# Second attention of an eight-image hybrid block: the token norm's root folded into the inner norm, values scaled behind their projection, GpSimd's work tied to the low copy

## What is computed

```python
t = _to_tokens(x)
t = t + _L1_attn_ref(_ln_t(t), ...)      # _ln_t: (v - mean) / sqrt(var + 1e-5), over the 128 channels
t = t + _L1_ffn_ref(_ln_t(t), ...)

def _L1_attn_ref(x, w_qkv, w_proj, qn_w, kn_w):
    EPS = 1e-06
    def _rmsnorm(x, w):
        y = xf * jax.lax.rsqrt(jnp.mean(xf * xf, axis=-1, keepdims=True) + EPS)
        return y * w
    qkv = x @ w_qkv.T
    q = _rmsnorm(heads(q), qn_w)          # mean over the two channels of a head
    k = _rmsnorm(heads(k), kn_w)
    att = jnp.einsum('bhtd,bhsd->bhts', q, k) * scale
    att = jnp.where(causal, att, -1e+30); att = jax.nn.softmax(att, axis=-1)
    return (att @ v) @ w_proj.T
```

## Time and profile before

| | us |
|---|---|
| median of 3 runs | 3653.44 (3650.4 to 3662.63) |
| the profiled execution, its own time | 3642.61 |
| its span in the profile | 3640.9 |
| first exponential of stage D starts | 994.8 |
| its last exponential ends | 3217.2 |

### The profile page before, as it was taken

One profiled execution on the slowest core, in us unless ns is written; L12 is line 12 of the kernel. 1 busy time (PEld: TensorE's weight loads), 2 busy tenths in 40 slices (PEclk: granted clock), 3 DMA queues, 4 the chain that ended last, 5 costly groups with the idle time before them and its releaser, 6 DMA issues.

```text
span 3640.9 us, 71108 instructions
## 1 busy us (share of the span) xinstructions
PE 3182.2 (87%) x27941; PEld 1144.4 (31%) x27941; DVE 2109.2 (58%) x3000; ACT 2727.1 (75%) x2577; POOL 296.9 (8%) x228
## 2 busy tenths in 40 slices
PE   5799999999398898898898898898898888979999
PEld 3344444444122222222222222222222222234443
DVE  3688888887347557457547546646646634432222
ACT  4444444444299999899999999899999999934555
POOL 5100000000200000101101101100100100010000
PEclk9899999999699999999999989999999999978999
DMA  5411212110100200210210200200210121000000
GB/s 186 125 44 50 51 45 49 42 42 11 45 16 17 57 25 19 55 25 16 55 26 18 55 25 16 55 25 18 46 34 16 25 48 43 19 11 6 14 12 14
DMA packets 134480, 136.78 MB, mean 38 GB/s; under 512 B 29102, under 2 KB 113164, under 8 KB 134156
## 3 DMA queue, kind: packets, MB, share of 16 engines
q1 hardware_dynamic: 134156, 132.29, 14.3%
HBM read 70.31 MB, written 55.57 MB: 35 GB/s over the span
## 4 chain that ended last, share of the span: by engine, by line
PE 45%; ACT 24%; issue 15%; DVE 11%; SPq 2%; POOL 2%; DMA 1%; DVEq 0%; ACTq 0%; POOLq 0%
ACT arena L896 23%; PE ps L1207 12%; PE ps L1167 5%; PE ps L1283 3%; PE ps L1290 3%; DVE arena L1591 3%; PE ps L1295 3%; PE ps L968 3%; PE ps L1015 3%; PE ps L1042 2%; PE ps L1017 2%; PE ps L1026 2%; PE ps L997 2%; SPq L499 1%; DVE arena L1373 1%
## 5 line engine op out<-in xcount | busy, mean ns | idle before, releaser
L896 ACT ACTIVATE arena<-ps 128x1536 f32<-128x1536 f32 x1536 | 2080.3, 1609 | 165.7 <-PE ps L1167 165.2
L1207 PE MATMUL ps<-arena 128*32 128x512 f32 (+3 forms) x12288 | 1305.4, 521 | 59.4 <-DVE arena L1591 59.4
L1591 DVE TENSOR_TENSOR arena<-arena,causal 128x512 f32<-128x512 f32 x1024 | 714.4, 739 | 368.5 <-ACT arena L896 359.5
L1167 PE MATMUL ps<-arena 15*128 15x512 bf16 (+3 forms) x6144 | 627.0, 340 | 198.3 <-ACT arena L896 152.8
L1167 PEld LDWEIGHTS ps<-arena 15*128 15x128 bf16 x6144 | 166.5, 92 | 1144.8 <-ACT arena L896 948.5
L840 ACT ACTIVATE arena<-ps 128x512 f32<-128x512 f32 x512 | 299.7, 595 | 267.2 <-PE ps L1017 256.8
L1207 PEld LDWEIGHTS ps<-arena 128*32 128x32 f32 x12288 | 289.2, 111 | 471.8 <-issue 349.1
L1373 DVE TENSOR_REDUCE arena<-ps 128x32 bf16<-128x1024 f32 x256 | 311.3, 1216 | 121.0 <-PE ps L997 121.0
L1380 DVE TENSOR_TENSOR arena<-arena,ps 128x512 f32<-128x512 f32 x512 | 329.2, 679 | 26.9 <-PE ps L1026 25.6
L1576 DVE COPY arena<-ps 128x512 f32<-128x512 f32 x256 | 176.5, 689 | 251.9 <-PE ps L1207 250.7
L1015 PE MATMUL ps<-arena 96*128 96x256 bf16 x1024 | 258.5, 277 | 0.3 <-ACT arena L816 0.2
(11 more groups left out here) (201 smaller groups left out, 2070.2 us busy)
## 6 DMA issues: line engine op xcount, KB each, us to landing
arena<-qstack SPq DMA_DIRECT2D x512, 30.0 KB
parts<-arena SPq DMA_DIRECT2D x8, 1536.0 KB, 5.9
arena<-parts SPq DMA_DIRECT2D x48, 256.0 KB, 5.6
arena<-parts SPq DMA_DIRECT2D x96, 128.0 KB, 2.8
arena<-kstack SPq DMA_DIRECT2D x512, 24.0 KB
qstack<-arena SPq DMA_DIRECT2D x48, 192.0 KB, 2.8
attn<-arena SPq DMA_DIRECT2D x512, 12.0 KB
arena<-arena SPq DMA_DIRECT2D x384, 16.0 KB, 1.8
```

The costliest lines, as they stand in the source:

```text
L896: act.activation(PR1[:, at:at + CW], bank(BPC * (f % 2), BPC), ACT.Exp).then_inc(d_exp, 1)
L1167: mm = pe.matmul(bank(at + k)[:, s * P:(s + n) * P], Ks[par][HR * h:HR * h + QROWS, j * P:(j + 1) * P], Qs[par][HR * h:HR * h + QROWS, t * ...
L1207: mm = pe.matmul(o[HR * h:HR * (h + 1), :], V1[n % 2][:, j, v:v + HR], pr[:, h * HALF + s * P:h * HALF + (s + k) * P], start=not opened[hi ...
L1591: dve.tensor_tensor(v, v, m3, ALU.min).then_inc(d_mask, 1)
```

## The change

With v the variance of a token and s the sum of squares of a head's two *unscaled* projections, the normed query is q / sqrt(s/2 + 1e-6 (v + 1e-5)): the outer root cancels and only its variance, times the inner epsilon, is left. So queries and keys are projected from the centred `xc`, and `vb`, the variance spread over a head's rows by two full matmuls, enters the inner root (`nrm[4]`, `eb`). The root of v is still needed for the values, which are projected from `xc` as well and multiplied by it, per token, when they are read out of bank 6: eight instructions of 128 columns per image in place of two copies of 512. turn, w0, w1 and the two multiplications by the widened root are gone for the next image; the projection side keeps its own.

- The tables are now by slot. Next image: m (group 0), q (1), k (2), vb and the first half of the variance by token (3), its second half (4), v (5). z for the image after next: group 6. The finished image: y (8), z (10), m (11), the variance halves in (12, 1) and (13, 0), turn and w0 (14), w1 and lg (15).
- Newton rounds of both token norms are done by GpSimd, four steps a round, 12 in a chain (`pool_root`); those of the inner norm stay on VectorE.
- `low_copied`: GpSimd waits for the low copy of group 1 before it squares `xc`, of 2 and 3 before queries' and keys' squares, of 9 before the products, of 12 before the squares of the finished image.
- Low planes are made by VectorE in group 11. The windows move up by one or two groups; the one of group 9 has the high planes and the first subtractions.
- SyncE stores the planes in group 11 in place of 12, and loads the attended values in group 0 in place of 2; the reciprocal of the divisors moves from group 4 to 2.
- Scratch space is taken from the planes' own words, behind a wait for their last stores.
- The first image's norm is rewritten to the same algebra; z0, z1 and the residual of image 1 are done in it.

```diff
+C_AT = {(0, 0): "m0", (0, 1): "m1", (1, 0): "q0", (1, 1): "q1", (2, 0): "k0", (2, 1): "k1", (3, 0): "vb",
+        (3, 1): "va0", (4, 0): "va1", (5, 0): "v0", (5, 1): "v1"}
+Z_AT = {(6, 0): "z0", (6, 1): "z1"}
+E_AT = {(8, 0): "y0", (8, 1): "y1", (10, 0): "z0", (10, 1): "z1", (11, 0): "m0", (11, 1): "m1", (12, 1): "va0",
+        (13, 0): "va1", (14, 0): "turn", (14, 1): "w0", (15, 0): "w1", (15, 1): "lg"}
...
+def use(g, slot):
+
+    n, gi = g // GPI, g % GPI
+    if (gi, slot) in C_AT and n + 1 < B:
+        return "C", n + 1, C_AT[gi, slot]
+    if (gi, slot) in Z_AT and n + 2 < B:
+        return "Z", n + 2, Z_AT[gi, slot]
+    if (gi, slot) in E_AT and n > 0:
+        return "E", n - 1, E_AT[gi, slot]
+    return None
...
-                if n + 1 < B and gi == 12:
-                    CG.after(sp, n, "lo3")
+                if n + 1 < B and gi == 11:
+                    CD.after(sp, n, "lo3")
                     store_stacks(n + 1)
...
+            def pool_root(steps, n, p, t_sem, first, v, y, t):
+
+                first()
+                for j in (1, 2, 3):
+                    if j > 1:
+                        steps.after(pool, n, f"{p}y{j - 1}")
+                    pool.tensor_tensor(t, y, y, ALU.mult).then_inc(t_sem, 1)
+                    steps.after(pool, n, f"{p}a{j}")
+                    pool.tensor_tensor(t, t, v, ALU.mult).then_inc(t_sem, 1)
+                    steps.after(pool, n, f"{p}b{j}")
+                    pool.tensor_scalar(t, t, -0.5, 1.5, ALU.mult, ALU.add).then_inc(t_sem, 1)
+                    steps.after(pool, n, f"{p}c{j}")
+                    pool.tensor_tensor(y, y, t, ALU.mult).then_inc(t_sem, 1)
...
+            def low_copied(g):
+
+                pool.wait_ge(d_ev, g * 2 + 1)
+
+            def pool_c(n):
+
+                m, g = n - 1, (n - 1) * GPI
+                low_copied(g + 1)
+                for th in range(2):
+                    CD.after(pool, m, f"xc{th}")
+                    pool.tensor_tensor(sq_h[th], xc_h[th], xc_h[th], ALU.mult).then_inc(c_pool, 1)
+                pool.wait_ge(c_stored, n * C_STORES * INC)
+                for j, last in enumerate(("ssq", "ssk")):
+                    low_copied(g + 2 + j)
+                    for k, to in ((2 * j, xn_h[j]), (2 * j + 1, scratch[j])):
+                        CD.after(pool, m, f"r{k}")
+                        pool.tensor_tensor(to, nrm[k], nrm[k], ALU.mult).then_inc(c_pool, 1)
+                    CG.after(pool, m, f"s{2 * j + 1}")
+                    pool.tensor_tensor(xn_h[j], xn_h[j], scratch[j], ALU.add).then_inc(c_pool, 1)
+                pool_root(CG, m, "d", c_pool, lambda: CD.after(pool, m, "dy0"), dv, dev, dtmp)
+                low_copied(g + 9)
+                CD.after(pool, m, "bound")
+                for k, to in enumerate((spare, xn_h[1])):
+                    pool.tensor_tensor(to, nrm[k], nrm[2 + k], ALU.mult).then_inc(c_pool, 1)
+                CG.after(pool, m, "p1")
+                pool.tensor_tensor(spare, spare, xn_h[1], ALU.add).then_inc(c_pool, 1)
+
             def pool_e(n):
+                if n + 1 < B:
+                    low_copied((n + 1) * GPI + 12)
                 for th in range(2):
                     ED.after(pool, n, f"xc{th}")
                     v = num[:, th * HALF:(th + 1) * HALF]
                     pool.tensor_tensor(esq[:, th * HALF:(th + 1) * HALF], v, v, ALU.mult).then_inc(e_pool, 1)
-
...
+                pool_root(EG, n, "e", e_pool, lambda: ED.after(pool, n, "ey0"), ev, edev, etmp)
...
-            def variance(squares, o, t_sem):
-
-                for t in range(NT):
+            def variance(squares, blocks, o, t_sem):
+
+                for t in blocks:
                     mm = pe.matmul(o[:, t:t + 1], squares[:, t * P:(t + 1) * P], mean_w[:, 0:1], start=True, stop=True)
                 mm.then_inc(t_sem, 1)
+
+            def variance_by_head(o, t_sem):
+
+                for th in range(2):
+                    mm = pe.matmul(o[NH1 * th:NH1 * (th + 1), :], mean_w[:, 0:NH1], sq_h[th], start=True, stop=True)
+                mm.then_inc(t_sem, 1)
...
-                    mm = pe.matmul(o[NH1 * th:NH1 * (th + 1), :], wt("qk1")[:, NH1 * k:NH1 * (k + 1)], xn_h[th],
+                    mm = pe.matmul(o[NH1 * th:NH1 * (th + 1), :], wt("qk1")[:, NH1 * k:NH1 * (k + 1)], xc_h[th],
...
+            def pe_c(n, name, o):
+
+                m = n - 1
+                if name in ("m0", "m1"):
+                    th = int(name[1])
+                    ZD.after(pe, m, f"x{th}")
+                    mean_of(n, th, o, c_pe)
+                elif name in ("q0", "q1", "k0", "k1"):
+                    CD.after(pe, m, "xc1")
+                    queries_keys(("q0", "q1", "k0", "k1").index(name), o, c_pe)
+                elif name == "vb":
                     CG.after(pe, m, "sq1")
-                    variance(sq, o, c_pe)
...
-                    values_of(th, o, c_pe)
+                    variance_by_head(o, c_pe)
+                elif name in ("va0", "va1"):
+                    th = int(name[2])
+                    CG.after(pe, m, "sq1")
+                    variance(sq, range(th * NT // 2, (th + 1) * NT // 2), o, c_pe)
                 else:
...
+                    CD.after(pe, m, "xc1")
+                    values_of(int(name[1]), o, c_pe)
...
+                elif name == "vb":
+                    dve.tensor_scalar(nrm[4], o, LN_EPS, RMS_EPS, ALU.add, ALU.mult).then_inc(c_dve, 1)
+                elif name in ("va0", "va1"):
+                    at = int(name[2]) * NT // 2
+                    dve.tensor_scalar(dv[:, at:at + NT // 2], o[:, at:at + NT // 2], LN_EPS, None, ALU.add)\
+                        .then_inc(c_dve, 1)
+                    if at:
+                        root_first(CD, m, "dv1", c_dve, dv, dev)
                 else:
-                    dve.tensor_copy(nrm[C_READ.index(name) - C_READ.index("r0")], o).then_inc(c_dve, 1)
+                    CG.after(dve, m, "dy3")
+                    for t in range(NT // 2):
+                        at = int(name[1]) * NT // 2 + t
+                        ins = dve.tensor_scalar(V1[n % 2][:, at, 0:3 * NH1].rearrange("p (h e) -> p h e", e=3)[:, :, 0:2],
+                                                o[:, t * P:(t + 1) * P].rearrange("p (h d) -> p h d", d=2),
+                                                dev[:, at:at + 1], None, ALU.mult)
+                    ins.then_inc(c_dve, 1)
...
+                    CD.after(dve, m, "eb")
+                    dve.scalar_tensor_tensor(xn_h[j], xn_h[j], 0.5, nrm[4], ALU.mult, ALU.add).then_inc(c_dve, 1)
+                    root_first(CD, m, p + "v", c_dve, xn_h[j], scratch[2 + j])
+                    root_round(CD, m, p, 1, c_dve, xn_h[j], scratch[2 + j], spare)
...
+                if gi == 3:
                     begun(0)
-                elif gi == 6:
+                elif gi == 4:
                     for j in (2, 3):
-                        root_round(CD, m, "q", j, c_dve, sq_h[0], xc_h[0], spare)
-                elif gi == 7:
+                        root_round(CD, m, "q", j, c_dve, xn_h[0], scratch[2], spare)
+                elif gi == 5:
                     normed(0)
                     normed(1)
+                elif gi == 6:
                     begun(1)
+                elif gi == 7:
+                    for j in (2, 3):
+                        root_round(CD, m, "k", j, c_dve, xn_h[1], scratch[3], spare)
                 elif gi == 8:
-                    for j in (2, 3):
-                        root_round(CD, m, "k", j, c_dve, sq_h[1], xc_h[1], spare)
-                elif gi == 9:
...
-                    CG.after(dve, m, "own")
-                    dve.wait_ge(c_stored, n * C_STORES * INC)
+                    dve.scalar_tensor_tensor(xn_h[0], xn_h[1], cv(c_ck + 1), xn_h[0], ALU.mult, ALU.add).then_inc(c_dve, 1)
+                elif gi == 9:
...
+                elif gi == 11:
+                    for k in five:
+                        CD.after(dve, m, f"mid{k}")
+                        r = hi_plane(k)
+                        dve.tensor_tensor(planes[:, r + 2, :], rst[k], planes[:, r + 1, :], ALU.subtract).then_inc(c_dve, 1)
```

360 lines of the change are left out of this document (159 added, 201 removed).

## The result

| | before | changed |
|---|---|---|
| median, us | 3651.92 (3644.97 to 3662.63, 4 runs) | 3535.28 (3533.61 to 3541.48, 4 runs) |
| profiled execution's span | 3640.9 | 3532.1 |
| stage D: first exponential to the end of the last | 2222.5 | 2121.9 |
| behind it | 423.7 | 426.3 |

The forecast of 3516 with its range of 3477 to 3572 and its sign were right; 19 us of the 136 did not come.

What follows compares the result with a forecast made beforehand. ScalarE's exponentials bound the second attention, with 177 us lost to clock falls and GpSimd-VectorE lock-step. Leaving 43 gains 134, plus 3.4 first norm, less 1.2 tail: 136 off the 3653.4 median, given as 3516 us, range 3477 to 3572.

Steps and rivals of the forecast that it cites:

- Parts 3 and 4: GpSimd held until low copies, low planes to VectorE: groups 5, 6, 10 regain 6.2 us, group 12 6.6, collisions cost 1.0.
- part 4: Low planes made by VectorE in group 11 (3.5 us more there); group 12 loses its 6.6 us excess.
- Parts 1 and 2: Next norm's widening goes, ending 5.7 us excess in groups 3 and 4; halved, moved variance costs 1.0, bounds 0 and 4.3.
- Part 7: Second projection half moved ahead, w1 and logits in group 15: costs 2.5 us an image, from 0 to 4.1 plus 2.9.
- Small misses: Allowance for unpriced loss in the stage: 0.5 us for each of images two to seven.
- Part 9: First norm, done once: the first long reciprocal starts earlier, gaining 3.4 us, bounds 0 and 6.
- Part 6: Token norms' Newton rounds on GpSimd, 0.2 us a step: hidden in the stream, 1.2 us lost in the tail.
- Part 5: Values scaled leaving PSUM, eight instructions of 0.17 to 0.35 us: 0.4 more than now per half, hidden in group 5.
- Part 8: SyncE's plane stores one group earlier, attended values loaded in group 0 instead of 2: cost 0.
- The rival of a clock that keeps falling: Clock falls at variance halves, w1 with logits, and after low-copy waits: 13 us lost per image, 3565 us; chance 0.20.
- Collisions: Rival: held GpSimd work delays masks in groups 3, 4 and 9, 4.2 us each, giving 3604 us; chance 0.05.
- the slow chain: Rival: VectorE in group 5 waits for 12 chained GpSimd Newton steps; at 3.2 us each 3675 us; chance 0.02.

Runs made afterwards that it cites:

- e1: Kernel before with only GpSimd's holds to the low copy added, and a finished image's squares put ahead of the planes: 3596.6 us, ratio 0.9829.
- e2: Changed kernel with GpSimd's waits for the low copy taken out: 3577.7 us, ratio 0.9782.
- e6: Changed kernel with the five low planes' differences back on GpSimd, held to the low copy of group 11: 3534.2 us, ratio 0.9672.
- e13: Kernel of e5 with the next image's variance whole in the second slot of group 4, in place of two halves: 3502.2 us, ratio 0.9598.
- e5: Kernel of e4 with three few-column pieces in groups 4, 13 and 15 moved from first to second slot: 3489.7 us, ratio 0.9551.
- e4: Changed kernel with router logits out of the stream, made once in the tail from images summed on GpSimd: 3519.6 us, ratio 0.9624.
- e10: Changed kernel with the router logits' 16 products 128 columns wide instead of 8, using other weights (output differs): 3517.9 us, ratio 0.9632.
- e9: Changed kernel with transposes in group 13's second slot, w0 and w1 in group 14, only router logits in group 15: 3517.0 us, ratio 0.9625.
- e7: Changed kernel with the three Newton rounds of each token norm back on VectorE: 3536.0 us, ratio 0.9689.
- e12: Kernel of e5 with the Newton rounds of the token norms back on VectorE, as in e7: 3504.7 us, ratio 0.9602.
- e3: Changed kernel with the next image's variance whole in group 4's first slot, in place of two halves: 3550.3 us, ratio 0.9689.

## Why the prediction was right, and where it was not

**Parts 3 and 4, the hold: right, with a wrong split.** 6.2 plus 6.6 less 1.0 was the forecast for an image; e1, with no hold on the products and a fall of the clock left in group 12, gives 7.6, and e2 takes 7.1 away. Groups 5 and 6 fell by 3.7, 10 by 1.5, 12 by 6.6, and the 0.5 each set aside for groups 3 and 9 were not needed. But part 4 gave the whole 6.6 of group 12 to the low planes and their move to VectorE. e6 shows that with the hold and the mids ready a group earlier, GpSimd does them for nothing, and e1 that 3.0 of the 6.6 stay with the hold alone, behind the finished image's variance, which the sum had no price for in that group. The change halved this variance and moved it to groups 12 and 13; no run takes that step alone. One reading was off: the squares that meet the masks in the earlier trace rows are those of the queries, not of the keys, whose turn comes a group later. The sum is not touched by it.

**Parts 1 and 2, clock after widening and variance: right.** The excess of groups 2, 3 and 4 over 15.98 was 8.0 in the mean of six images (10.0 in the sixth, from which the terms were read) and is 0.7. The two halves of variance in the first slots of 4 and 13 cost 0.4 + 1.9 = 2.3 for the 2.0 forecast. That halving matters is shown by e13 (12.5 us for one piece), that the first slot matters too by e5 (30 us for three pieces).

**Part 7, w1 and logits in group 15: the step that failed.** It had 2.5 an image, from bounds 0 and 7.0, with the reason that no wait stands ahead of the logits now. The measured price is 4.2 in group 15 and 1.3 in group 0, together 5.5 (from unrounded lengths), and with the group 0 that follows 7.1 to 7.3 behind images two to five. The wait of 0.54 stands ahead of w1, and w1 brings the fall that the logits then keep up: w1 without logits costs 1.9 in groups 15 and 0 (e4), with wide ones 2.1 (e10), the logits away from w1 1.8 (e9), the two together 5.5. The first slot of every group has this wait for the low copy; it should have been laid beside each piece of narrow work. Six images of 3.0 are 18 us of the 33 that are missing in the stage.

**Small misses and the ends.** 0.5 an image was set aside; the rest of the sixteen groups (1 to 3, 5 to 12, 14, each 0.0 to 0.4 over 15.98) comes to about 1.9, 8 us more in six images, and the 1.0 for collisions did not come, 6 us less. The first image was to lose 3.6 and lost 8.5, the last 3.5 and lost 10.1, 11.5 more together: in both a run of groups stood at 17.0 (below). The whole account: 136 less 33 in the stage, 3 more at the first norm, 1 less behind the stage and 4 from the first attention, which no part had, is the 109 of the profiled spans, 27 short of the forecast. The medians' 117 is 8 more, as the profiled execution of before is a quick one; that the miss is only 19 by them is partly luck.

**Part 9, first norm: the sign right, the size over its bound.** 6.4 against 3.4 with bounds 0 and 6. The chain of the changed kernel against the earlier trace rows:

```profile
925.53 1.98 PE ps L1091 x4
927.51 1.72 PE ps L1088 x4
929.23 3.58 PE ps L1102 x16
...
933.67 1.89 PE ps L1078 x16
...
937.36 6.57 DVE arena L1465 x2
```

Queries and keys take 3.58 us where they took 5.15, at a granted clock of 1.00 in place of 0.71, and the variance 1.89 in place of 2.54, which gives 2.2 of the 3.0 above the forecast. Variance, transpose and widening, narrow and with waits between them, no longer stand ahead; that this kept the clock is likely and was not tried. The long reciprocals start 10.8 us earlier than the 948.20 of before, 4.4 of it from the first attention.

**Part 6, Newton on GpSimd: right in the stream, low in the tail.** A step takes 0.20 us, as taken, but the next starts 0.27 to 0.30 later:

```profile
3133.74 0.20 POOL L737 TENSOR_TENSOR arena<-arena 128x8 f32<-128x8 f32 x1 [2.60 <-DVE arena L1483]
3134.02 0.20 POOL L739 TENSOR_TENSOR arena<-arena 128x8 f32<-128x8 f32 x1
```

Twelve take 3.4 us, nine on VectorE at 0.20 apart 1.8 (e7): 1.6 for the 1.2 forecast. Behind the stage 2.6 were lost in all, of which e7 takes 1.0 back; the rest was not traced. The Trainium skill (GPSIMD Engine Reference, When to use GPSIMD) has GpSimd about two times slower than VectorE for elementwise operations with two inputs. The trace here has 0.20 to 0.17 in duration and 0.28 to 0.20 in spacing at this size, less than two.

**Part 5** was at the upper bound: the eight scalings of an image take 345 ns each (L1521) where 0.17 to 0.35 was given; all but hidden, as group 5's 16.3 shows. **Part 8**: 0, the wait for stacks is 45.8 us at the stage's start, 45.2 before.

The rival of a clock that keeps falling (0.20, 3565, 13 us an image) had the right mechanism for what is left and the wrong size: 9.6 an image, 5.5 of it at w1 and the logits. Collisions and the slow chain did not come.

## What to carry to other kernels

Where the engine that makes the bottleneck's input has a slack stretch in every round, hold the helper engine's bulk work to that stretch with one wait per piece: it gave 43 of the 109 us here, and which of the two engines made the low planes mattered 1 us. Lay TensorE's narrow products (one column, eight columns, eight partitions) in short pieces where no wait stands before or behind them. Here 1.05 us of it behind a wait of 0.55, or 1.95 us of it with no wait, let the clock fall for the values behind in most images, and 1.04 us of idle time alone did not. When steps are placed in slots, price each slot with the wait that it has, not only with the step that goes in.

## What was not expected of the hardware

**A fall that repeats itself.** In the first image of the changed kernel no projection work stands in groups 8 to 15. Groups 8 to 11 take 17.0 with a clock of 0.90, 12 to 14 take 15.96 with 1.00, on nearly the same TensorE work:

```profile
1150.20:1167.21 17.01, 14.80 (x148) 3.55 (x144) 10.49 (x20) 16.33 (x13) 0.00 (x0) 0.90 0.07 17
1167.21:1184.22 17.01, 14.80 (x152) 3.56 (x144) 9.48 (x15) 16.33 (x13) 0.00 (x0) 0.91 0.07 16
1184.22:1200.18 15.96, 13.05 (x148) 3.50 (x144) 6.56 (x10) 15.96 (x13) 0.00 (x0) 1.00 0.52 116
```

A group that has had one fall is 17.01 long, and the clock falls again at the same point of the next group (to 0.50 for 3.4 us at 1132.7, 1149.7 and 1166.8 us), several times over; then it stops. The last image of the changed kernel (groups 4 to 6, 17.0 each) and e12 and e13 show it too. VectorE's work for the next image also ends with group 11 in the first image, but the series of the last image has no such work beside it and stops all the same. What starts and ends such a series was not tried.

**Falls trade places.** Taking one away in group 15 (e4) brought another in group 4; the changed kernel itself has it there in two images of seven, 17.7. And the same work behind the same wait need not bring a fall. In group 13 of the kernel before, w0 (L1060) stands in the first slot behind the low copy, and the group takes 16.0 in five of the six images; in e1, with the same order on TensorE, it falls in most. The sixth image of before, then of e1:

```profile
2626.73 0.93 PE L1060 MATMUL ps<-arena,sel 8*128 8x128 f32 x6 [0.55 <-DVE arena L1576]
...
2628.03 1.07 PE L1207 MATMUL ps<-arena 128*32 128x512 f32 x8
```

```profile
2580.21 0.93 PE L1067 MATMUL ps<-arena,sel 8*128 8x128 f32 x6 [0.54 <-DVE arena L1583]
...
2581.75 1.94 PE L1214 MATMUL ps<-arena 128*32 128x512 f32 x8
```

So narrow work behind a wait makes a fall likely, not certain, and what decides is open. With e3's spread of 25 us between runs of one kernel, this says that a place near the edge must be judged by several images and runs, not by one.
